# Double-buffered routing scratch, one register load per expert block and a refitted time table in a two-layer attention and expert kernel

## The reference, cut to what matters

```python
xn = layernorm(x)
x = x + L0_attn(xn) + L0_ffn(xn)      # 16 heads, causal, keys and values from a 32-wide latent
xn = layernorm(x)                      # L0_ffn: 8 experts, the two best of each row, softmax gates
x = x + L1_attn(xn) + L1_ffn(xn)       # L1_attn: three attentions in a chain
# L0_ffn
sel = top_2(xn @ Wg + bg);  gates = softmax(where(sel, logits, -inf))
out = sum_e gates[e] * (relu(xn @ W1[e] + b1[e]) @ W2[e] + b2[e])
# L1_attn
ctx = attention(16 heads of 8, scores * sigmoid gate)
ctx = 0.3 * ctx + 0.7 * mha(xn, 4 heads);  ctx = 0.85 * ctx + 0.15 * mha(ctx, 4 heads)
# L1_ffn
h = silu(xn @ w1) * (xn @ w2);  h = gelu(h @ h1);  h = gelu(h @ h2);  out = h @ w3
```

## Time and profile before

| | us |
|---|---|
| median of 3 runs | 1735.37 |
| lowest, highest run | 1732.73, 1735.88 |
| profiled execution, from its first to its last instruction | 1744.8 |
| PE busy in it | 1542.1 |
| DVE, ACT, POOL busy in it | 1199.4, 1055.2, 792.1 |

### The profile page before, as it was taken

The page is one execution under the profiler, slowest core; times in us unless marked ns, Lnnn a source line. Parts: engine busy times, 40 slices in busy tenths (PEclk is TensorE's granted clock), DMA queues, the critical chain, the costliest instruction groups (busy, mean ns, idle before and its releaser), DMA issues.

```text
span 1744.8 us, 34024 instructions
## 1 busy us (share of the span) xinstructions
PE 1542.1 (88%) x11497; PEld 656.0 (38%) x11497; DVE 1199.4 (69%) x3135; ACT 1055.2 (60%) x2322; POOL 792.1 (45%) x725
## 2 busy tenths in 40 slices
PE   3586898999999999998999999999999999889878
PEld 1353453245333543345333543345324533232232
DVE  7554478567875788667885788677876677476523
ACT  2372475667656765676666765677657765636442
POOL 5246345535645456354644455354644461501120
PEclk9998699999999999999999999999999999989877
DMA  7652451136212631136212621145212620201010
GB/s 277 205 153 69 135 158 36 57 109 176 63 34 77 167 102 48 63 115 159 63 34 87 180 79 52 62 135 145 58 46 82 186 78 7 62 15 35 1 37 6
DMA packets 138875, 159.35 MB, mean 91 GB/s; under 512 B 15744, under 2 KB 100304, under 8 KB 137808
## 3 DMA queue, kind: packets, MB, share of 16 engines
q1 hardware_dynamic: 134608, 148.79, 29.4%
q0 software_dynamic: 4096, 8.40, 1.6%
HBM read 115.96 MB, written 40.85 MB: 90 GB/s over the span
## 4 chain that ended last, share of the span: by engine, by line
PE 61%; DVE 13%; ACT 9%; issue 6%; POOL 6%; DMA 3%; SPq 2%; ACTq 0%; POOLq 0%; DVEq 0%
PE banks L454 58%; DVE negmax L879 6%; ACT probs L1222 3%; ACT hm L1291 3%; POOL psums L1443 2%; POOL xslots L1417 1%; DMA qkc<-relm 1%; DVE h L1103 1%; ACT L1222 1%; PE banks L731 1%; POOL halves L1399 1%; PE banks L684 1%; SPq L1579 1%; ACT h L1340 1%; POOL yg L1432 0%
## 5 line engine op out<-in xcount | busy, mean ns | idle before, releaser
L1222 ACT ACTIVATE probs<-banks 128x512 f32<-128x512 f32 (+3 forms) x1216 | 582.1, 535 | 371.7 <-PE banks L454 352.9
L879 DVE TENSOR_REDUCE negmax<-banks 128x1 f16<-128x512 f32 x768 | 492.2, 685 | 159.5 <-PE banks L454 156.5
L875 DVE CUSTOM_DVE_ANT_0 scr<-banks,mask_row 128x384 bf16<-128x384 f32 (+3 forms) x512 | 230.2, 487 | 150.9 <-PE banks L454 149.1
L454 PE MATMUL banks<-kp,qs 32*128 32x512 f16 (+3 forms) x1024 | 239.7, 360 | 60.4 <-DVE negmax L875 23.5
L454 PE MATMUL banks<-probs,vp 128*32 128x512 f32 (+3 forms) x2048 | 241.0, 544 | 0.2 <-POOL probs L1395 0.2
L454 PE MATMUL banks<-qs,kp 32*128 32x512 f16 (+3 forms) x1024 | 218.5, 352 | 23.2 <-ACT probs L1222 15.9
L1483 POOL TENSOR_TENSOR h_lo<-h,h_hi 128x512 f16<-128x512 f32 x96 | 114.4, 1209 | 246.4 <-ACT h_hi L1334 150.8
L1423 POOL TENSOR_TENSOR hl<-hm,hh 128x512 f16<-128x512 f32 x120 | 139.7, 1166 | 131.7 <-DVE hh L1045 131.7
L1291 ACT ACTIVATE hm<-banks,wt 128x128 f32<-128x128 f32 x480 | 137.8, 374 | 77.4 <-PE banks L454 77.0
L454 PE MATMUL banks<-qkc 97*128 97x512 f16 (+1 forms) x512 | 168.5, 402 | 8.7 <-DVE negmax L879 3.0
L454 PEld LDWEIGHTS banks<-kp,qs 32*128 32x128 f16 x1024 | 63.1, 92 | 277.5 <-DVE negmax L879 109.8
(11 more groups left out here) (212 smaller groups left out, 2462.0 us busy)
## 6 DMA issues: line engine op xcount, KB each, us to landing
wt<-wexp SPq DMA_DIRECT2D x120, 258.0 KB, 3.1
wt<-wexp SPq DMA_DIRECT2D x120, 256.0 KB, 3.0
qkc<-relm SPq DMA_DIRECT2D x96, 128.0 KB, 3.2
qs<-relq SPq DMA_DIRECT2D x64, 128.0 KB, 2.3
kp<-relk SPq DMA_DIRECT2D x64, 128.0 KB, 2.3
relm<-halves SPq DMA_DIRECT2D x32, 256.0 KB, 2.1
xg<-xslots SPq DMA_DIRECT2D x24, 256.0 KB, 3.0
yslots<-yv SPq DMA_DIRECT2D x24, 256.0 KB, 3.6
```

Of the source, the lines that this page charges most:

```text
L454: return nc.tensor.matmul(psum[rows_, bank, cols_], lhsT, rhs, start=start, stop=stop)
L875: v.tensor_tensor_reduce(scr[:, s, 0:kw], psum[:, SCO + s, 0:kw], mask_row[:, T - kw:T], -1.0, 3e38, ALU.add, ALU.min, negmax[:, g.n % 2, ...
L879: v.tensor_reduce(negmax[:, g.n % 2, NC * h + c:NC * h + c + 1], psum[:, SCO + s, 0:kw], AX.X, ALU.max, negate=True).then_inc(sem("max"), 1)
L1222: a.activation(keys(g, c)[:, 2 * pair + s, q0:T], psum[:, TRA + s, q0:T], ACT.Exp, scale=SCALE[main(g)]).then_inc(sem("exp"), 1)
```

## The change

1. The routing scratch exists twice, indexed by b % 2: `owner`, `idx`, `gk`, `gates`. The waits on the batch before become waits on the batch before that, and only from b = 2 on.
2. `cmp2` has memory of its own. `cmp1` lies in `hh` for batch 0 only, and for later batches over the `ca_q` and `ca_k` columns of the weights in full precision, which are dead once `l1_split` has run. `rank0` no longer waits for `down`.
3. `l1_split` moves from position 14 to -19 (of stage "front", so -18 in batch 0).
4. `load_up` keeps its register and `load_down` of the same block uses it; the second load of `owner` is gone.
5. Some 100 of the positions in `AT` and `MOVE` are new, most by one or two.

```diff
-MOVE = {"route": {0: 6}, "warm0": {-1: -6}, "warm1": {-1: 6}, "front": {}, "keys": {0: -8, 1: -5}, "joined": {0: 3}, "prep": {0: 13},
+MOVE = {"route": {0: 7}, "warm0": {1: -2, 2: 2, -3: -1, -2: -4, -1: -5}, "warm1": {0: -2, 1: -1, 2: -1, -1: 6}, "front":
+        {0: 1}, "keys": {0: -8, 1: -5}, "joined": {0: 3}, "prep": {0: 13}, ...
-"l1_split": 14, ... "q0r": -32, "q0r_out": -31, ... "pos": -29, ... "pick": -10, ... "gT": 39, "gT_out": 40,
+"l1_split": -19, ... "q0r": -31, "q0r_out": -30, ... "pos": -30, ... "pick": -16, ... "gT": 38, "gT_out": 39,
-"x1_stat": 63, "x1_root": 65, "x1_norm": 66, ... "mod": 72, "q1_out": 75, "q1_low": 75, "k1_out": 76, "k1_low": 75,
+"x1_stat": 62, "x1_root": 64, "x1_norm": 65, ... "mod": 71, "q1_out": 74, "q1_low": 76, "k1_out": 75, "k1_low": 77,
-"ctx": 181, ... "mck_low": 210, "mck_send": 213, "mc_spread": 217, ... "mc_mul": 250, "mc_o_out": 255, "ctx2": 256, "store": 257
+"ctx": 185, ... "mck_low": 209, "mck_send": 211, "mc_spread": 213, ... "mc_mul": 251, "mc_o_out": 254, "ctx2": 255, "store": 256
-AT.update({("h0", i): at for i, at in enumerate((28, 36, 43, 51), 0)})
+AT.update({("h0", i): at for i, at in enumerate((26, 36, 43, 52), 0)})
-AT.update({("h1_out", i): at for i, at in enumerate((152, 157, 167, 180), 0)})
+AT.update({("h1_out", i): at for i, at in enumerate((151, 159, 168, 180), 0)})
-AT.update({("wup", i): at for i, at in enumerate((5, 7, 7, 10, 12, 15, 17, 19, 21, 25, 25, 25, 29, 31, 33), 0)})
+AT.update({("wup", i): at for i, at in enumerate((5, 7, 7, 9, 12, 15, 18, 19, 22, 26, 26, 26, 30, 33, 34), 0)})
-AT.update({("y_store", i): at for i, at in enumerate((20, 29, 37, 43), 0)})
+AT.update({("y_store", i): at for i, at in enumerate((22, 34, 39, 44), 0)})
-AT.update({("warm0", i): at for i, at in enumerate((34, 37, 43, 47, 51, 55, 56, 57, 66, 68), 0)})
-AT.update({("warm1", i): at for i, at in enumerate((178, 181, 186, 188, 192, 192, 194, 194, 197, 199), 0)})
+AT.update({("warm0", i): at for i, at in enumerate((35, 39, 42, 46, 48, 55, 58, 62, 71, 70), 0)})
+AT.update({("warm1", i): at for i, at in enumerate((177, 180, 185, 188, 192, 192, 196, 198, 198, 198), 0)})
-AT.update({("gelu2_hi", i): at for i, at in enumerate((167, 167, 168, 168), 0)})
-AT.update({("gelu2_low", i): at for i, at in enumerate((168, 168, 169, 169), 0)})
+AT.update({("gelu2_hi", i): at for i, at in enumerate((166, 166, 168, 168), 0)})
+AT.update({("gelu2_low", i): at for i, at in enumerate((167, 168, 168, 168), 0)})
...
-        owner = sb("owner", [1, NT + 1], I32)
+        owner = sb("owner", [1, 2, NT + 1], I32)
-        idx = sb("idx", [P, 2 * NC], U32)
-        gk = sb("gk", [P, 2, NC])
+        idx = sb("idx", [P, 2, 2 * NC], U32)
+        gk = sb("gk", [P, 2, 2, NC])
-        gates = sb("gates", [P, NC, E])
-        cmp1, cmp2 = (hh[:, k, :].bitcast(F32).rearrange("p (c e f) -> p c e f", e=E, f=E) for k in range(2))
+        gates2 = sb("gates2", [P, 2, NC, E])
+        cmp2 = sb("cmp2", [P, NC, E, E])
+        dead, _ = WIDE_AT["ca_q"]
+
+        def compared(b):
+            at = wide[:, dead:dead + NC * E * E] if b else hh[:, 0, :].bitcast(F32)
+            return at.rearrange("p (c e f) -> p c e f", e=E, f=E)
...
                     if k == 0:
-                        if b:
-                            dve.wait_ge(sem("down"), NT * b)
...
-                        if b:
-                            full(dve, "m", "gT", b - 1)
+                        if b >= 2:
+                            full(dve, "m", "gT", b - 2)
...
-                    if b:
-                        dve.wait_ge(sem("gath"), 128 * b)
+                    if b >= 2:
+                        dve.wait_ge(sem("gath"), 128 * (b - 1))
...
-                    if b:
-                        dve.wait_ge(sem("down"), NT * b)
+                    if b >= 2:
+                        dve.wait_ge(sem("down"), NT * (b - 1))
...
-                    if b:
-                        dve.wait_ge(sem("scaled"), 2 * b)
+                    if b >= 2:
+                        dve.wait_ge(sem("scaled"), 2 * (b - 1))
...
-                    e = sp.value_load(owner[0:1, t:t + 1], min_val=0, max_val=E - 1)
+                    e = expert_of[n] = sp.value_load(owner[0:1, b % 2, t:t + 1], min_val=0, max_val=E - 1)
...
-                    e = sp.value_load(owner[0:1, t:t + 1], min_val=0, max_val=E - 1)
+                    e = expert_of.pop(n)
```

More of the change, by code:

```diff
@@ L81 @@
 A1_AT = (120, 128, 136, 152)
[L83 to L84 removed]
+MOVE = {"route": {0: 7}, "warm0": {1: -2, 2: 2, -3: -1, -2: -4, -1: -5}, "warm1": {0: -2, 1: -1, 2: -1, -1: 6}, "front":
+        {0: 1}, "keys": {0: -8, 1: -5}, "joined": {0: 3}, "prep": {0: 13}, "ca": {-1: -24}, "mid": {-1: -24},
+        "last": {-1: -30}, "ffn": {-1: -24}, "tail": {-2: -12, -1: -52}}
 @dataclass
@@ L113, in groups_in_order @@
     return out
[L116 to L120, removed]
[3 rows of a table removed]
[L124 to L129, removed]
@@ L130 @@
-AT.update({("spread0", i): at for i, at in enumerate((-7, -5, 5, 17), 0)})
-AT.update({("spread1", i): at for i, at in enumerate((110, 117, 126, 142), 0)})
-AT.update({("h0", i): at for i, at in enumerate((28, 36, 43, 51), 0)})
+AT = {"l1_split": -19, "x_load": -59, "x_stat": -50, "x_root": -50, "x_norm": -48, "xT0": -39, "xT0_out": -38, "xr_hi": -44,
+      "xr_lo": -38, "lat": -36, "lat_stat": -36, "lat_root": -34, "lat_norm": -33, "latT": -33, "latT_out": -32, "q0":
+      -34, "q0_out": -33, "q0r": -31, "q0r_out": -30, "q0_sum": -30, "q0_send": -27, "k0": -19, "k0_out": -18, "k0r":
+      -16, "k0r_out": -14, "k0_sum": -15, "k0_send": -10, "rank0": -35, "rank1": -32, "rank2": -33, "gex": -31,
+      "gates": -29, "pos": -30, "starts": -27, "slots": -25, "addresses": -25, "pick": -16, "v0a": 3, "v0a_out": 4,
[3 rows of a table added]
+      "caq": 77, "caq_out": 78, "caq_low": 78, "caq_send": 79, "cak": 79, "cak_out": 79, "cak_low": 82, "cak_send":
+      83, "ca_spread": 109, "cav": 112, "cav_out": 113, "v1": 129, "v1_out": 130, "bo": 101, "ca_div": 136, "ca_mul":
+      141, "ca_o": 142, "ca_o_out": 145, "gelu1": 151, "gelu2": 166, "f3": 171, "f3_out": 173, "f3_add": 172, "back1":
+      181, "ctx": 185, "mcq": 205, "mcq_out": 205, "mcq_low": 206, "mcq_send": 207, "mck": 207, "mck_out": 208,
+      "mck_low": 209, "mck_send": 211, "mc_spread": 213, "mcv": 220, "mcv_out": 221, "mc_div": 249, "mc_mul": 251,
+      "mc_o": 254, "mc_o_out": 254, "ctx2": 255, "wo1": 256, "wo1_out": 256, "store": 256}
@@ L133 @@
+AT.update({("spread0", i): at for i, at in enumerate((-7, -5, 5, 16), 0)})
+AT.update({("spread1", i): at for i, at in enumerate((110, 117, 128, 146), 0)})
+AT.update({("h0", i): at for i, at in enumerate((26, 36, 43, 52), 0)})
 AT.update({("h0_out", i): at for i, at in enumerate((28, 37, 44, 52), 0)})
-AT.update({("h1", i): at for i, at in enumerate((151, 157, 166, 179), 0)})
-AT.update({("h1_out", i): at for i, at in enumerate((152, 157, 167, 180), 0)})
+AT.update({("h1", i): at for i, at in enumerate((151, 157, 166, 180), 0)})
@@ L140 @@
-AT.update({("scatter", i): at for i, at in enumerate((-16, -15, -16, -15), 0)})
-AT.update({("gather", i): at for i, at in enumerate((45, 46, 48, 49), 0)})
-AT.update({("xg_load", i): at for i, at in enumerate((-5, -4, 7, 19), 0)})
+AT.update({("down", i): at for i, at in enumerate((13, 15, 17, 18, 21, 23, 25, 27, 31, 32, 33, 35, 37, 39, 42), 0)})
+AT.update({("wup", i): at for i, at in enumerate((5, 7, 7, 9, 12, 15, 18, 19, 22, 26, 26, 26, 30, 33, 34), 0)})
+AT.update({("wdn", i): at for i, at in enumerate((8, 12, 13, 14, 17, 19, 22, 23, 26, 27, 30, 32, 34, 35, 38), 0)})
@@ L143 @@
+AT.update({("scatter", i): at for i, at in enumerate((-17, -16, -16, -15), 0)})
+AT.update({("gather", i): at for i, at in enumerate((45, 46, 49, 49), 0)})
+AT.update({("xg_load", i): at for i, at in enumerate((-7, -5, 6, 19), 0)})
 AT.update({("xg", i): at for i, at in enumerate((7, 15, 23, 31), 0)})
 AT.update({("xg_out", i): at for i, at in enumerate((7, 15, 23, 31), 0)})
-AT.update({("y_out", i): at for i, at in enumerate((19, 28, 36, 42), 0)})
-AT.update({("y_store", i): at for i, at in enumerate((20, 29, 37, 43), 0)})
@@ L151 @@
+AT.update({("warm1", i): at for i, at in enumerate((177, 180, 185, 188, 192, 192, 196, 198, 198, 198), 0)})
 AT.update({("scale", i): at for i, at in enumerate((52, 51), 0)})
-AT.update({("split", i): at for i, at in enumerate((-12, -11, -2, 3, 7, 21, 35), 0)})
-AT.update({("load", i): at for i, at in enumerate((1, 14, 25), 4)})
+AT.update({("split", i): at for i, at in enumerate((-13, -11, -4, 3, 8, 21, 39), 0)})
+AT.update({("load", i): at for i, at in enumerate((1, 15, 26), 4)})
 AT.update({("fa", i): at for i, at in enumerate((133, 135, 137, 139), 0)})
@@ L157 @@
 AT.update({("glu", i): at for i, at in enumerate((135, 137, 139, 142), 0)})
-AT.update({("glu_low", i): at for i, at in enumerate((136, 138, 140, 143), 0)})
+AT.update({("glu_low", i): at for i, at in enumerate((135, 138, 140, 143), 0)})
```

(8 more changed lines are left out.)

27 lines of the change are left out of this document (15 added, 12 removed), and 6 rows, old and new, of the table AT.

## The result

| kernel | median, us | runs | lowest to highest |
|---|---|---|---|
| before | 1738.1 | 20 | 1732.29 to 1744.71 |
| after | 1730.84 | 20 | 1724.28 to 1738.97 |

The ratio of after to before is 0.9963, 95% interval 0.995 to 0.9976, so 4.2 to 8.7 us less: 6.4 by the ratio, 7.3 by the medians. The forecast was 7.1 us less.

The account below looks back on a forecast made before the run. PE, 88% busy, was taken as the bound. Gains of 15.9 us less losses of 8.8 gave 7.1 us net, taken off a 1735.4 us median: 1728.3 us, the forecast's own range 1723 to 1731, the whole range 1712 to 1741.

Parts of the forecast that it names:

- Waits that double buffering removes: `rank0`, `addresses` and `pick` no longer wait on the batch before: gain 0, bounds 0 and 1.25 us.
- one register load: SP saves one register load for each of 120 blocks, shortening PE's waits for transfers: gain 1.0 us, bounds 0 and 4.4.
- `q1_out`, 9.0 and 2.7 for the clock: Position 75 to 74: PE's wait before `k1` goes, 9.0 us; half clock behind it goes in two of eight batches, 2.7.
- `k1_out`, 1.5: Position 76 to 75: in batch 0 it stands ahead of the relu, ending the wait of `caq`; gain 1.5 us.
- `l1_split`, 1.7: Position 14 to -19: PE's 1.74 us idle behind it goes, its new place hidden by PE's wait for gathered rows; gain 1.7 us.
- `h0`, 4.0 lost: Group 0 from 28 to 26: PE waits 0.5 us for DVE's copy of the max rows in each of 8 batches.
- `pick`, 2.4 lost: Position 70 to 64: its 1.12 us of DVE delays the next eviction; 0.4 us lost in each of 6 batches.
- `h1_out`, 1.5 lost: Group 0 from 72 to 71, ahead of the reduction a filler burst waits for; 0.25 us lost in 6 batches.
- Three bursts at the end, 0.9 lost: Three filler bursts, where one stood, right ahead of the `wo1` of batch 7: 0.9 us lost, bounds 0 and 1.4.
- `gelu2_hi`, left out: Blocks 0 and 1 to position 166: up to 12 us less DVE time, not counted as no PE wait was found behind it.
- Rival 2: The wait moves on: PE waits at the next units instead, +2.6 us, 1735 to 1738 us; chance 0.20.
- Rival 3: Slower: the wait for bank M at `h0` brings PE's clock down in 8 batches, +6.4 us, 1742 us; chance 0.20.

Follow-up runs that it names:

- b1_split: Kernel before with `l1_split` alone moved from 14 to -19, old `q1_out` kept; median 1741.8 us, ratio to before 1.0003.
- a1_q1: Kernel before with one number changed, `q1_out` at 74 instead of 75; median 1720.18 us, ratio to before 0.9919.

## Why the prediction came out right, step by step

The net came out right (7.1 us forecast, 4.2 to 8.7 measured), but that it came so close is in good part luck: the steps were too small and too large at once. `q1_out` and the program brought more than was priced, the earlier half of the table cost 12.5 us, where the prediction had priced 4.9 us of losses there (`h0` and the bursts) and a gain of 1.7, and the 3.9 us for `pick` and `h1_out` weren't there. The time itself, 1730.84 us against 1728.3 forecast, lies near the upper end of the range (1731), since the three runs behind the 1735.4 lay 2.7 us below the median of twenty.

- *Waits that double buffering removes, 0; one register load, 1.0.* The two together gave 3.5 us (-0.7 to 7.8). The waits behind it fell by 3.8 of the 4.4 us of the bound; I took too little, if anything, though the interval reaches past zero.
- *`q1_out`, 9.0 and 2.7 for the clock.* 14.1 us alone, 11.8 within the change; 11.7 lies in both intervals. The wait was what I took it for. The term for the clock wasn't sound: the fall behind the wait, read in one batch, is there in four of eight in the profile of before, in one of eight in b1_split, and taking it away with filler gave 1.2 us (at most 4.9).
- *`k1_out`, 1.5.* The wait of 1.95 us in batch 0 is 0.66 us now (1.2 us of line 1256's 1.8 lie at 1113 us, in a batch where none was). By its own it wasn't measured.
- *`l1_split`, 1.7.* In its place 2.2 us, and nothing left of it in the whole time.
- *`h0`, 4.0 lost.* 4.3 us of waits, 3.0 us by the runs. Right in mechanism and size.
- *`pick`, 2.4 lost; `h1_out`, 1.5 lost.* This step failed. Moving `pick` back gave nothing (0.9972 against 0.9963), and moving `h1_out` back as well cost 17.6 us. I counted their 1.1 and 0.5 us of DVE as if they pushed only what stands behind them, in the old order of the rest. Their new positions belong with the other new ones and can't be priced alone.
- *Three bursts at the end, 0.9 lost.* From the mixing output to the last `wo1` it is now 1721.07 - 1717.52 = 3.55 us; in the profile of before it was 1740.18 - 1737.55 = 2.63. So 0.92 us, in one profile of each. The twelve matmuls:

```profile
1718.48 2.75 PE L467 MATMUL banks<-ident 128*128 128x512 f16 x12
1721.07 1.05 PE L467 MATMUL banks<-wide,ctxT 128*128 128x128 f32 x8
```

- *`gelu2_hi`, left out.* All 64 casts of `gelu1_hi` and `gelu2_hi` together, before and after:

```profile
L1111 DVE CAST h_hi<-h 128x512 f16<-128x512 f32 x64 | 38.8, 649 | 0.3 <-ACT h L1340 0.3
```

```profile
L1125 DVE CAST h_hi<-h 128x512 f16<-128x512 f32 x64 | 28.0, 480 | 9.8 <-ACT h L1354 9.8
```

  38.8 us became 28.0, so 10.8 us of DVE where the prediction had 12 from its rows and the rule of the Trainium skill, "SBUF — State Buffer", section "Who interferes with whom". The last two casts take 0.75 us in place of 2.28. PE gained nothing from it at that place, as I had found no wait behind it: from the last score unit ahead of the casts to the fourth behind them it is 10.49 us before (1336.18 to 1346.67) and 10.50 after (1323.61 to 1334.11).
- *Not foreseen.* The waits for `r_b` (2.7 to 5.6 us) and for `hm` (11.5 to 14.5 us), and the start: expert weights 2.95 us late. I had written that the rest of the positions change nothing on the path. `r_b` (2.9) and `h0` (4.3) make 7.2 of the 12.5 us that the earlier half of the table costs; the rest of it I can't place. That is a sum of waits set beside a difference of times, and the waits weren't each taken away alone.

Rival 2 was right in one sign, and it is one that the prediction had named as showing the forecast wrong: PE's idle time didn't fall (65.1 to 68.0 us in five batches, 13.0 to 13.6 a batch) although the wait for line 1074 is gone. As a sign it didn't hold, for the kernel is faster all the same. But it isn't the same time moved on; a1_q1, with `q1_out` alone, keeps its gain (PE's waits in all 177.1 against 185.7 us), and it is other positions that add new waits. Rival 3 had the right place and no fall of the clock behind it: the transposes behind that wait take 0.63 us with it and 0.66 without, and they are at full clock in all eight batches.

## What to carry to other kernels

When a table of positions is fitted as a whole, take it apart again: one number (`q1_out`) held more than all of the gain, and half of the table cost 12.5 us. And price no clock term from one place in one profile: where the clock falls changes from one profile to the next. A wait is worth what its removal brings forward behind it; filling it with work that nobody needs brought nothing, even where the clock then stayed up. And a wait that comes once, as the power behind eight scatters, can be worth as much as one in each batch: the list of waits sorted by the longest shows it, that by count doesn't.

## What the runs showed of the hardware

Executions of one kernel differ by about 22 us here (1728 to 1750 us in 73 of the kernel before), and so does a single profile: with ratios known to 0.1 to 0.3%, steps of 1 to 3 us can be read from waits but not from times. A DVE subtraction of 128x1024 took 2.16 us beside a sum of POOL and 1.20 us without; two casts of 128x512 tiles took 2.28 and 0.75 us. After the same idle time of 1.24 us PE's clock was at half in some batches and profiles and at full in others. A read of one number into a register of SP took 0.27 us, and at the longest 1.15.
